# A stencil layer's tail: GpSimd takes the kept part's product, dt times the field moves to PSUM, and four banks hold the results

## What is computed

```python
# first layer: x = x + sum over the two chosen experts of gate * (relu(h @ w1 + b1) @ w2 + b2)
def _L1_cond_ref(f, A_grid, B_grid, dt):
    Af = A_grid[None] * f[:, None]
    Bf = B_grid[None] * f[:, None]
    gradv_Af = _grad(Af[:, 0], 1) + _grad(Af[:, 1], 2)
    gradvv_Bf = _grad2(Bf[:, 0], 1) + _grad2(Bf[:, 1], 2) + _grad(_grad(Bf[:, 2], 2), 1) + _grad(_grad(Bf[:, 2], 1), 2)
    df = -gradv_Af + gradvv_Bf * 0.5
    f_new = f + df * dt[:, None, None]
    return jnp.maximum(f_new, 0.0)
```

## Time and profile before

| | us |
|---|---|
| median of 3 runs | 379.67 (378.07 to 381.65) |
| the profiled execution, its own time | 380.79 |
| its span, first to last instruction | 378.9 |
| mean granted clock of PE | 0.932 of full speed |
| first matmul of the tail / last one's end | 328.96 / 375.6 |

### The profile page before, as it was taken

The page is one execution under the profiler, slowest core; times in us unless marked ns, Lnnn a source line. Parts: engine busy times, 40 slices in busy tenths (PEclk is TensorE's granted clock), DMA queues, the critical chain, the costliest instruction groups (busy, mean ns, idle before and its releaser), DMA issues.

```text
span 378.9 us, 7113 instructions
## 1 busy us (share of the span) xinstructions
PE 319.7 (84%) x2312; PEld 287.1 (76%) x2312; DVE 289.4 (76%) x523; ACT 253.5 (67%) x467; POOL 142.1 (37%) x108
## 2 busy tenths in 40 slices
PE   1674414799999999998999999999999894299996
PEld 1554414699999999997999999999999894143342
DVE  4697691678787787878787888788777890799994
ACT  2577214397797797679878889879877951459211
POOL 1235403152535655443445565545534414101000
PEclk9999655599999999998999999999999999589999
DMA  8902333983777867565777777756667401997411
GB/s 280 342 29 83 112 112 137 281 260 118 261 251 253 276 205 266 198 235 186 256 260 263 250 243 246 236 185 248 238 223 250 143 4 35 326 223 166 112 55 55
DMA packets 49924, 74.83 MB, mean 197 GB/s; under 512 B 3309, under 2 KB 40559, under 8 KB 49776
## 3 DMA queue, kind: packets, MB, share of 16 engines
q1 hardware_dynamic: 45056, 62.13, 48.7%
q0 software_dynamic: 4512, 12.07, 10.9%
q10 hardware_dynamic: 336, 0.39, 0.3%
HBM read 63.56 MB, written 9.31 MB: 192 GB/s over the span
## 4 chain that ended last, share of the span: by engine, by line
PE 28%; DMA 23%; ACT 16%; DVE 15%; issue 11%; SPq 3%; POOL 2%; ACTq 1%; DVEq 0%; POOLq 0%
DMA raw_a<-in_L_cond_exp_w_dram 17%; PE psum L935 8%; PE psum L887 8%; PE psum L909 6%; ACT relu L579 5%; DVE w_split L1180 5%; ACT w_split L556 4%; DMA x_sb<-t_y 2%; ACT hid L588 2%; PE psum L843 1%; ACT w_split L549 1%; DMA t_y<-y_rows 1%; DVE st L1004 1%; SPq L403 1%; POOL rs L712 1%
## 5 line engine op out<-in xcount | busy, mean ns | idle before, releaser
L725 POOL DMA_INDIRECT gathered<-h_rows,src_cur x40 | 71.5, 1787 | 130.4 <-DVE src_cur L1169 75.7
L909 PE MATMUL psum<-w_split,hid 128*128 128x256 f32 x936 | 117.8, 285 | 0.4 <-issue 0.4
L909 PEld LDWEIGHTS psum<-w_split,hid 128*128 128x128 f32 x936 | 113.6, 192 | 0.6 <-issue 0.6
L887 PE MATMUL psum<-slot_h,w_split 128*128 128x256 f32 x768 | 99.2, 290 | 4.9 <-DVE slot_h L1186 4.8
L887 PEld LDWEIGHTS psum<-slot_h,w_split 128*128 128x128 f32 x768 | 97.0, 199 | 6.1 <-issue 6.1
L1180 DVE TENSOR_TENSOR w_split<-raw_b,w_split 128x2048 fp32r<-128x2048 f32 x23 | 52.7, 2292 | 21.8 <-ACT w_split L556 18.6
L1174 DVE TENSOR_TENSOR w_split<-raw_a,w_split 128x2048 fp32r<-128x2048 f32 x23 | 52.7, 2290 | 16.9 <-ACT w_split L549 9.5
L549 ACT ACTIVATE w_split<-raw_a 128x2048 fp32r<-128x2048 f32 x23 | 44.2, 1922 | 26.1 <-DMA raw_a<-in_L_cond_exp_w_dram 26.1
L588 ACT ACTIVATE hid<-relu 128x512 fp32r<-128x512 f32 (+1 forms) x92 | 50.9, 590 | 12.1 <-DVE relu L1192 12.1
L738 POOL DMA_INDIRECT y_rows<-y_sb,dst_cur x39 | 48.8, 1251 | 26.4 <-DVE y_sb L1222 10.8
L579 ACT ACTIVATE relu<-psum,b_cur 128x256 f32<-128x256 f32 x128 | 52.6, 484 | 1.2 <-PE psum L887 0.7
(11 more groups left out here) (167 smaller groups left out, 356.8 us busy)
## 6 DMA issues: line engine op xcount, KB each, us to landing
raw_a<-in_L_cond_exp_w_dram SPq DMA_DIRECT2D x23, 1024.0 KB
raw_b<-in_L_cond_exp_w_dram SPq DMA_DIRECT2D x23, 1024.0 KB
t_y<-y_rows SPq DMA_DIRECT2D x6, 512.0 KB, 8.1
x_sb<-t_y POOLq DMA_DIRECT2D x5, 512.0 KB, 4.9
x_sb<-in_x_dram SPq DMA_DIRECT2D x4, 512.0 KB, 7.2
h_rows<-h_tok SPq DMA_DIRECT2D x16, 128.0 KB, 2.2
out_dram<-t_out SPq DMA_DIRECT2D x3, 512.0 KB, 2.9
b_all<-in_L_cond_exp_b_dram SPq DMA_DIRECT2D x1, 1024.0 KB, 10.1
```

Source lines behind the costliest of these rows:

```text
L725: pool.indirect_dma_start(out=gathered[:, par, t, :], out_offset=None, in_=h_rows, in_offset=bass.IndirectOffsetOnAxis(ap=src_cur[:, par, ...
L887: last = pe.matmul(banks[bank][:, ST * (blk % 2):ST * (blk % 2) + rows], w_split[:, 0, par, w, at:at + P], slot_h[:, par, h, k, 0:rows], s ...
L909: last = pe.matmul(banks[bank][:, D * t:D * t + D], hid[:, par, h, blk, P * t:P * t + P], w_split[:, 1, par, w, D * blk:D * blk + D], star ...
```

## The change

- DVE keeps only center(0). POOL does center(1) to center(3) (`tensor_tensor`, 128 x 1024, f32), and for pairs 1 and 2 it then adds GF to SM (`merge`), in SBUF.
- PE has no "kept" block for pairs 1 and 2 any more, since the merged SM carries it; b0f starts these sums. PE's "cols" block of pair g-1 now stands between b0f(g) and u(g), and it waits for POOL's merge (`t_s_pool`) for pairs 1 and 2.
- FD lies in PSUM, banks 4 and 5 or 6 and 7 by the parity of g. ACT writes it and five wide and two short DVE products of a pair read it.
- The results share banks 0 to 3 by the parity of g, so PE waits for relu_out(g-2) (`t_relu`) before it starts a sum of pair 2 or 3.
- DVE's wait for `t_mm` stands before products(g) instead of center(g). ACT's order of instructions is unchanged.

```diff
-            FD, GG, GF, PA, PB, CC, U1, U2, PP, PQ, SM, OUT = (
+            GG, GF, PA, PB, CC, U1, U2, PP, PQ, SM, OUT = (
...
+            FD = [psum[:, 4 + 2 * par:6 + 2 * par, :].rearrange("p b n -> p (b n)") for par in range(2)]
...
+        MERGED = (1, NPAIR - 1)
...
-                               psum[:, 2 * g:2 * g + 2, :].rearrange("p q (i d) -> p q i d", i=2),
+                               psum[:, 2 * (g % 2):2 * (g % 2) + 2, :].rearrange("p q (i d) -> p q i d", i=2),
...
-                if g >= 2:
-                    act.wait_ge(t_gf, g - 1)
+                if g == 2:
+                    act.wait_ge(t_gf, 1)
+                elif g > 2:
+                    act.wait_ge(t_gf_pool, g - 2)
...
+            def center(g):
+                if g == 1:
+                    pool.wait_ge(t_f, 2)
+                else:
+                    pool.wait_ge(y2_added[g], 16)
+                pool.wait_ge(t_keep, g + 1)
+                if g == 2:
+                    pool.wait_ge(t_mm, 1)
+                pool.tensor_tensor(GF[g % 2], GG[g % 2], field(g), ALU.mult).then_inc(t_gf_pool, 1)
+
+            def merge(g):
+                pool.wait_ge(t_s, g + 1)
+                pool.wait_ge(t_gf_pool, g)
+                pool.tensor_tensor(SM[g % 2], SM[g % 2], GF[g % 2], ALU.add).then_inc(t_s_pool, 1)
+
+            add_y1(1)
+            add_y1(2)
+            center(1)
+            add_y2(2)
+            add_y1(3)
+            center(2)
+            merge(1)
+            add_y2(3)
+            pool.wait_ge(t_s_pool, 1)
+            center(3)
+            merge(2)
...
-            for g in range(NPAIR + 1):
-                if g >= 1:
-                    pe.wait_ge(t_s, g)
-                    for q in range(2):
-                        last = rows_mm(g - 1, q, ident, SM[(g - 1) % 2], q, stop=True)
-                        if g == NPAIR or q == 1:
-                            last.then_inc(t_mm, 1)
...
+            for g in range(NPAIR):
+                merged = MERGED[0] <= g < MERGED[1]
+                if g >= 2:
+                    pe.wait_ge(t_relu, g - 1)
+                if not merged:
...
+                pe.wait_ge(t_u2, g + 1)
+                along_rows(g, C_D2, U2, start=merged)
+                if g >= 1:
+                    columns(g - 1)
+                pe.wait_ge(t_u1, g + 1)
+                along_rows(g, C_D1, U1)
+            columns(NPAIR - 1)
...
             for g in range(NPAIR):
-                center(g)
+                if g == 0:
+                    center_first()
```

More of the change, by code:

```diff
@@ L271, in moe_then_stencil @@
             F0, FV = ([own(f"{n}_0", [P, 4 * D])[:, :]] for n in ("t_f0", "t_f"))
-            FD, GG, GF, PA, PB, CC, U1, U2, PP, PQ, SM, OUT = (
+            GG, GF, PA, PB, CC, U1, U2, PP, PQ, SM, OUT = (
                 [own(f"{n}_{par}", [P, 4 * D])[:, :] for par in range(2)]
-                for n in ("t_fd", "t_keep", "t_kept", "t_a0f", "t_b2f", "t_d1b2f",
+                for n in ("t_keep", "t_kept", "t_a0f", "t_b2f", "t_d1b2f",
                           "t_u1", "t_b0f", "t_pf", "t_qf", "t_cols", "t_out"))
+            FD = [psum[:, 4 + 2 * par:6 + 2 * par, :].rearrange("p b n -> p (b n)") for par in range(2)]
             edge_p = own("edge_p", [P, 2, 2, 4, 2, 4])
@@ L332, in moe_then_stencil @@
         t_keep, t_fd, t_gated = sem("t_keep"), sem("t_fd"), sem("t_gated")
+        t_gf_pool, t_s_pool = sem("t_gf_pool"), sem("t_s_pool")
         out_dma = [sem(f"out_dma{i}") for i in range(3)]
@@ L689, in _ @@
                 act.activation(OUT[(NPAIR - 1) % 2].rearrange("p (i q d) -> p q i d", i=2, q=2)[:, q],
-                               banks[2 * NPAIR - 2 + q].rearrange("p (i d) -> p i d", i=2),
+                               banks[2 * ((NPAIR - 1) % 2) + q].rearrange("p (i d) -> p i d", i=2),
                                ACT.Relu).then_inc(t_relu, 1)
@@ L755, in _, with add_y1, add_y2 @@
             scatter(NS - 1, None, halves=True)
-            for g in range(1, NPAIR):
+            def add_y1(g):
                 pool.wait_ge(t_gated, 2 * g - 1)
                 pool.dma_start(field(g), Y1[g], accum_op=ALU.add).then_inc(y1_added[g], 16)
[L760 to L763, removed]
+            def add_y2(g):
+                pool.wait_ge(t_gated, 2 * g)
+                pool.wait_ge(y1_added[g], 16)
+                pool.dma_start(field(g), Y2[g], accum_op=ALU.add).then_inc(y2_added[g], 16)
+            def center(g):
[22 more added lines that the diff above has]
+            merge(2)
         @block.tensor
@@ L934, in rows_mm @@
                 v = v.rearrange("p (i q d) -> p q i d", i=2, q=2)
-                return pe.matmul(banks[2 * g + q].rearrange("p (i d) -> p i d", i=2), w, v[:, k, :, :],
+                return pe.matmul(banks[2 * (g % 2) + q].rearrange("p (i d) -> p i d", i=2), w, v[:, k, :, :],
                                  start=start, stop=stop)
@@ L942, in along_rows, with columns @@
                         rows_mm(g, q, cst[:, at:at + P], u[g % 2], k, start=start and k == 0)
-            for g in range(NPAIR + 1):
-                if g >= 1:
-                    pe.wait_ge(t_s, g)
-                    for q in range(2):
-                        last = rows_mm(g - 1, q, ident, SM[(g - 1) % 2], q, stop=True)
-                        if g == NPAIR or q == 1:
-                            last.then_inc(t_mm, 1)
-                if g < NPAIR:
-                    pe.wait_ge(t_gf, g + 1)
+            def columns(g):
+                if MERGED[0] <= g < MERGED[1]:
+                    pe.wait_ge(t_s_pool, g)
+                else:
+                    pe.wait_ge(t_s, g + 1)
+                for q in range(2):
+                    last = rows_mm(g, q, ident, SM[g % 2], q, stop=True)
+                    if g == NPAIR - 1 or q == 1:
+                        last.then_inc(t_mm, 1)
+            for g in range(NPAIR):
[4 more added lines that the diff above has]
+                    if g == 0:
+                        pe.wait_ge(t_gf, 1)
+                    else:
+                        pe.wait_ge(t_gf_pool, g)
                     for q in range(2):
                         rows_mm(g, q, ident, GF[g % 2], q, start=True)
[L955 to L958, removed]
+                pe.wait_ge(t_u2, g + 1)
[5 more added lines that the diff above has]
+            columns(NPAIR - 1)
         @block.vector
@@ L1329, in rows_of, with center_first @@
                 return v.rearrange("p (r d) -> p r d", d=D)
[L1331 to L1340, removed]
+            def center_first():
+                dve.wait_ge(t_f, 1)
+                dve.wait_ge(t_keep, 1)
+                dve.tensor_tensor(GF[0], GG[0], field(0), ALU.mult).then_inc(t_gf, 1)
             def products(g):
@@ L1344, in products @@
                 f, a, b = FD[par], PA[par], PB[par]
+                if g >= 2:
+                    dve.wait_ge(t_mm, g - 1)
                 dve.wait_ge(t_fd, g + 1)
```

## The result

| | before | after |
|---|---|---|
| median, us | 380.44 (4 runs) | 390.11 (386.83 to 390.79, 4 runs) |
| span of the profiled execution | 378.9 | 388.1 |
| first matmul of the tail to the end of the last | 328.96 to 375.6: 46.6 | 329.30 to 384.8: 55.5 |

The ratio of after to before is 1.0245, 95% interval 1.0166 to 1.0324: slower by 9.3 us. The expert layer's part varies by up to 3.6 us from run to run (the first matmul of the tail stands between 328.1 and 331.7 us in the traces of this case), so where one profile is laid beside another I use the last line of the table, the length of the tail. It grew by 8.9 us. Executions over 1.5% above the fastest of their kernel are left out of every ratio here: 3 of the 12 of e1, 1 of the 10 of e3, and 2 of the 17 of the kernel before beside e5 and e7.

A forecast was written before the change was run, and what follows sets the result against it. PE was to bound the tail without a break from b0f(2), which late FD(2) delays: 3.35 us of wait plus 3.4 us of clock loss, 6.75 over a median of 379.67, gives 386.4 us; 8-in-10 range 383.0 to 390.0.

The forecast's parts named there:

- The moved block is what ACT waits for: Tail, PE to ACT: cols(0) behind b0f(1) delays relu_out(0), gated(3) and FD(2), so DVE's b2f(2) starts 2.7 us late.
- +3.35 us from the wait: Tail's end: late FD(2) starts b0f(2) at 358.08, then PE runs unbroken to 378.93 against 375.59.
- The clock, twice 1.7 us: PE behind its two new idle stretches: 1.2 GHz for some 3.4 us each, costing 1.7 us twice, +3.4 us.
- the 6.75 forecast: Whole kernel: total predicted slowdown in us, 3.35 from the wait plus 3.4 from the clock.
- POOL costs nothing: POOL's five wide tail instructions: 2.2 us each, all hidden, adding nothing to the sum.
- the 2.7 from which it would decide: Rival on POOL: wide instructions over 2.7 us delay DVE's SM(2) and b2f(3), mostly 387 to 391 us; chance 0.13.
- PSUM as DVE's source at nothing: DVE's products reading FD from PSUM: 684 ns for 512 columns with or without PSUM input, so no cost.
- DVE's three products give 2.3 us: DVE's tail queue: three products fewer at 1.14 us each, pair 1's gaining nothing, leaving 2.3 us if nothing else is late.
- The signs: Expected in the changed profile: PE idle before b0f(1) and b0f(2), clock 0.5 behind each, ACT and DVE idle, POOL near 2.2 us.

The follow-up runs named there:

- e1: Changed kernel with PE's cols(0) back ahead of b0f(1); ratio 0.9994 to the kernel before, -0.2 us.
- e3: Changed kernel with ACT's gated(g+2) swapped ahead of relu_out(g-1); ratio 1.0044 to the kernel before, 1.7 us over.
- e5: e1 with FD back in SBUF; ratio 1.0259 to the kernel before, 9.9 us over.
- e7: Changed kernel with cols(0) and cols(1) ahead of the U2 wait, only pair 2 merged, center(3) held until U1(2) is done; ratio 0.9981 to the kernel before.
- e4: Kernel before with only PE's cols(g-1) moved behind b0f(g); ratio 1.0164 to the kernel before, 6.2 us slower.
- e2: Changed kernel plus ten useless PE matmuls, five ahead of each wait for U2(1) and U2(2); ratio 1.0105 to the kernel before, 4.0 us over.

## Why the prediction was right

- *The moved block is what ACT waits for.* Right. After PE's start of b0f(1), `t_mm` came 7.8 us later, and from there to the end of FD(2) it took 5.4 us (352.58 to 357.99), the 5.42 that the prediction adds up. e1 takes the loss away by the place of cols(0) alone, e4 makes most of it by that alone, e3 takes most of it away at ACT's end of the same wait.
- *+3.35 us from the wait.* Right: with the clock held, e2 is 4.0 us over, 3.6 without the 0.39 us that only it has. A slip in the sum: 3.70 + 40 x 0.43 is 20.90 and not 20.85, which moves the term by 0.05.
- *The clock, twice 1.7 us.* The mechanism was right, the term too small; this is the step that was mis-sized. b0f(1) took 6.03 us for 3.70, so 2.3 lost, and b0f(2) 6.50, so 2.8: 5.1 together where 3.4 were forecast. e2 gets 4.8 of it back, which is 5.1 less the 0.39 us that only e2 has. The prediction took 3.4 busy us at 1.2 GHz behind each idle stretch; it was 4.7 and 5.7, the second at its upper bound. The first idle stretch was also longer than worked out, 5.11 us for 3.8, in good part because in this execution the clock rose earlier in pair 0 and u(0) was over at 339.7. The clock makes 1.7 of the 2.1 us between the 6.75 forecast and the tail's 8.9. So the median of 390.1 came out just above the top end of the range (390.0) and not at 386.4. It stands beside a median of 380.44 for the kernel before; on the 379.67 that the prediction had, the ratio gives 389.0, inside the range.
- *When the clock fell* makes the difference in size. In the changed kernel it fell while PE was still idle (342.7, 359.8), and the slow stretch lasted 6.8 us each time. In e1, e3, e4 and the first time in e5 it held through the whole idle stretch, fell 0.1 to 1.3 us behind its end and came back after some 3.4 us: that is the 1.7 us of the prediction (5.40 for 3.70). What decides between the two, no run here shows.
- *POOL costs nothing.* Right. Its instruction takes 2.35 us (I took 2.2), under the 2.7 from which it would decide. It did keep SM(2) back by 1.07 us (0.7 by the prediction), and DVE still waited 2.37 us for FD(3). The Trainium skill's GPSIMD Engine Reference, section 3.1, has 4497 ns for an add of 2048 columns; the estimate of 2.25 us from it agrees with the 2.35 to within 5%.
- *PSUM as DVE's source at nothing.* Right: 1.21 us for a PSUM product, 1.22 for one from SBUF. (The two rows are a sum and a difference, not products.) ACT's write of FD to PSUM is 0.68 us a half, 0.04 less than to SBUF. What the prediction did not see is that this move carries the change: without it POOL and DVE block each other, and e5 is as slow as the changed kernel for quite another reason.
- *DVE's three products give 2.3 us.* They give nothing in the changed kernel, where DVE waits for ACT, and nothing measurable in e1. There PE was only 0.7 us a pair behind DVE from the start and is the next bound at once, and since cols(1) still stands behind b0f(2), 48 records follow from there where 44 did before. e7, which puts cols(1) ahead and leaves 44, is 1.0 us shorter in its profile. No run takes the three products away alone, so this part is argued.
- *The signs.* Those that rest on order came as named: both idle stretches of PE ended by U2, the clock at 1.2 GHz behind each, ACT idle on PE, DVE idle on ACT, PE without a gap from b0f(2) on. The lengths were mostly at or past the far end: PE idle 5.11 us (3 to 4), ACT 9.10 (7), DVE 6.12 and 2.37 (4 to 6 and 1 to 2).

## What to carry to other kernels

Before a block is moved behind a wait, ask who waits for its result, and what stands queued behind that one: here two matmuls were put behind 5.1 us of waiting and a block of 6.0, and the price was paid on ACT, by FD(2), which has nothing to do with them. Work taken off PE can be work that covered its waits; when the cover goes, the slower clock can come on top, and here it cost more (5.1 us) than the wait itself (3.6). When GpSimd is to work beside VectorE, look at each VectorE instruction that it meets and give it one input from PSUM: that is the whole difference between e1 (-0.2 us) and e5 (9.9).

## What the hardware showed that was not expected

- An idle stretch of PE of over 3 us cost 1.7 to 2.8 us again behind it: blocks of 3.6 to 3.7 us took 5.40 (idle before: 3.10, 3.41, 3.62, 4.66 us), 5.80 (4.65), 6.03 (5.11) and 6.50 (4.92), while 1.06, 1.59 and 1.74 us of idleness left them at 3.67 to 3.70. Two idle stretches of the same length, 4.65 and 4.66, are followed by 5.80 and 5.40. In the expert layer, 1.80 us were enough, in a stretch in which PE was busy 1.50 of 3.30 us. So the length of the idle stretch alone says neither whether the clock falls nor what that costs. The clock can also hold through the whole idleness and fall behind it; in e1, where PE was idle from 340.3 to 345.0:

```profile
340.30:345.00 4.70, 0.05 (x1) 1.00 0.09 17
345.00:346.00 1.00, 0.99 (x1) 0.53 1.02 197
```

- A VectorE product with both inputs in SBUF that meets a GpSimd one stretches up to 3.37 us in the trace (from 1.22), with no idle time before it: the wait hides in a busy row.
